# Where TensorE turns the second half of the next chunk in a feed-forward stage

## The reference

```python
def _binarize(w):
    alpha = jnp.mean(jnp.abs(w), axis=1, keepdims=True)
    bw = alpha * jnp.sign(w)
    return w + jax.lax.stop_gradient(bw - w)
def _L0_ffn_ref(x, w1, b1, w2, b2):
    h = jnp.einsum('bsd,hd->bsh', x, _binarize(w1)) + b1
    h = jax.nn.gelu(h, approximate=False)
    return jnp.einsum('bsh,dh->bsd', h, _binarize(w2)) + b2
x = x + 0.5 * _L0_ffn_ref(_layernorm(x), L0_ffn_w1, L0_ffn_b1, L0_ffn_w2, L0_ffn_b2)
```

## Time and profile before

| what | value |
|---|---|
| median of 3 runs | 2248.06 us (2246.12 to 2248.31) |
| the profiled execution's own time | 2251.7 us |
| its span | 2249.8 us |
| PE busy | 1971.8 us (88%) |
| DVE busy | 1643.4 us (73%) |
| ACT busy | 1222.4 us (54%) |
| POOL busy | 497.4 us (22%) |
| `down` of the first block to that of the last, first stage | 52.30 to 178.96 |
| the same, second stage | 694.93 to 818.36 |

### The profile page before, as it was taken

One profiled execution on the slowest core, in us unless ns is written; L12 is line 12 of the kernel. 1 busy time (PEld: TensorE's weight loads), 2 busy tenths in 40 slices (PEclk: granted clock), 3 DMA queues, 4 the chain that ended last, 5 costly groups with the idle time before them and its releaser, 6 DMA issues. The chain is left out here.

```text
span 2249.8 us, 74481 instructions
## 1 busy us (share of the span) xinstructions
PE 1971.8 (88%) x32248; PEld 1256.2 (56%) x32248; DVE 1643.4 (73%) x2668; ACT 1222.4 (54%) x1870; POOL 497.4 (22%) x804
## 2 busy tenths in 40 slices
PE   2897898989897975989869999999999999999985
PEld 2664565656565654558735555555555555555543
DVE  7675556555656778767567888888888888888847
ACT  2673332323236754233227777677776777677754
POOL 3000000000000000000124544345434444445410
PEclk7998999989898976999859999999999999999997
DMA  4000000000000010434583555445453555455312
GB/s 142 1 1 1 21 2 21 3 20 3 20 3 1 1 31 1 132 124 183 186 251 101 143 143 142 130 119 142 128 139 106 142 150 143 116 134 136 100 30 75
DMA packets 273791, 195.11 MB, mean 87 GB/s; under 512 B 206744, under 2 KB 260310, under 8 KB 273210
## 3 DMA queue, kind: packets, MB, share of 16 engines
q1 hardware_dynamic: 262586, 139.27, 24.4%
q0 software_dynamic: 10496, 50.75, 6.0%
q10 hardware_dynamic: 384, 0.33, 0.0%
HBM read 91.69 MB, written 93.88 MB: 82 GB/s over the span
## 5 line engine op out<-in xcount | busy, mean ns | idle before, releaser
L2214 DVE TENSOR_REDUCE a1c_nm<-a1c_S 128x1 f32<-128x1024 f32 x512 | 609.6, 1218 | 84.8 <-PE a1c_S L2301 84.3
L2148 ACT ACTIVATE a1c_PT<-a1c_ST 128x1024 f32<-128x1024 f32 x499 | 510.3, 1023 | 69.0 <-PE a1c_ST L2301 66.2
L2165 ACT ACTIVATE a1c_Pb<-a1c_S,a1c_nm 128x192 f32<-128x192 f32 (+1 forms) x512 | 212.8, 416 | 201.8 <-DVE a1c_nm L2214 200.7
L2087 POOL TENSOR_TENSOR a1c_lt<-a1c_lt 128x256 f32<-128x256 f32 (+5 forms) x448 | 254.7, 568 | 35.4
L2204 DVE COPY a1c_PbT<-a1c_T 96x512 f32<-96x512 f32 x256 | 175.7, 686 | 100.3 <-PE a1c_T L2333 97.9
L2301 PE MATMUL a1c_ST<-a1c_Q,a1c_KR 57*128 57x256 f16 (+2 forms) x1066 | 176.5, 286 | 31.6 <-ACT a1c_PT L2148 19.6
L2301 PE MATMUL a1c_S<-a1c_KL,a1c_Q 54*32 54x512 f16 (+11 forms) x3136 | 193.4, 326 | 0.3
L2301 PE MATMUL a1c_S<-a1c_KR,a1c_Q 54*32 54x512 f16 (+13 forms) x2816 | 181.9, 317 | 12.2 <-DMA a1c_Gx<-a_bias 9.5
L2301 PE MATMUL a1c_S<-a1c_Gx,ident 64*32 64x96 f32 (+2 forms) x4352 | 186.1, 242 | 0.0
L2079 POOL DMA_DIRECT2D a_band<-a1c_Pb x128 | 71.4, 558 | 496.1 <-ACT a1c_Pb L2165 496.0
L1150 POOL PARTITION_ALL_REDUCE b_wall<-b_wsum x2 | 0.8, 407 | 813.3 <-DVE b_wsum L1195 813.3
(11 more groups left out here) (366 smaller groups left out, 3983.1 us busy)
## 6 DMA issues: line engine op xcount, KB each, us to landing
a_band<-a1c_Pb POOLq DMA_DIRECT2D x128, 384.0 KB, 3.5
a_bias<-a1b_G SPq DMA_DIRECT2D x32, 768.0 KB, 9.2
a1c_Gx<-a_bias SPq DMA_DIRECT2D x128, 192.0 KB, 4.4
a1c_Dt<-a_band SPq DMA_DIRECT2D x128, 126.0 KB, 3.7
a1c_Q<-a_qk SPq DMA_DIRECT2D x192, 64.0 KB
a1c_Vw<-a_values SPq DMA_DIRECT2D x64, 102.0 KB, 2.7
a1c_KL<-a_qk SPq DMA_DIRECT2D x96, 64.0 KB
a1c_KR<-a_qk SPq DMA_DIRECT2D x90, 64.0 KB
```

The source lines that it names most:

```text
L2087: add = lambda o, x, y: nc.gpsimd.tensor_tensor(o, x, y, ALU.add)
L2148: nc.scalar.activation(PT[:, q % 8, :, :], place(q), ACT.Exp).then_inc(s["exp"], 1)
L2165: nc.scalar.activation(Pb[:, band_slot(I, c), w0:w1], SP[:, t % 2, I * P - 32 + w0:I * P - 32 + w1], ACT.Exp, bias=nm[:, t // 16 % 2, col: ...
L2214: nc.vector.tensor_reduce(nm[:, t // 16 % 2, col:col + 1], SP[:, t % 2, :], AX.X, ALU.max, negate=True).then_inc(s["max"], 1)
```

## The change

In PE's loop the call that turns the second half of the next chunk stands behind round 2 in place of round 1, that is behind `down(8i + 2)` and `hidden(8i + 5)`. It holds for both stages. Nothing else changes: the waits inside `transposed`, and the lists of ACT and DVE, stay as they are.

```diff
                 if m == MH - 1 and i + 2 < NC:
                     transposed(i + 2, 0)
-                if m == 1 and i + 1 < NC:
+                if m == 2 and i + 1 < NC:
                     transposed(i + 1, 1)
```

## The result

The changed kernel takes 2227.53 us (median of 4 runs, 2224.73 to 2232.91) against 2247.55 (the median with a fourth run of the kernel before): ratio 0.9913, 95% interval 0.9897 to 0.9928. The forecast was 2227.5. Two later measurements gave medians of 2232.19 and 2231.00 us and ratios of 0.9927 (0.9909 to 0.9945) and 0.9919 (0.9901 to 0.9937), so the gain is 17 to 20 us by the medians, and that the first one meets the forecast to 0.03 us is luck.

The account below looks back on a forecast made before the run. PE was taken to bound both FFN stages, not quite full because it pauses at the turn for `xlo`. 17.4 + 3.2 = 20.6 us off the median 2248.06 gave 2227.5 us, range 2223.5 to 2236.5.

Parts of the forecast that it names:

- Step 1: Ordinary chunks of both FFN stages: PE's pause at the second half's turn goes, 1.34 us in each of 13 chunks, 17.4 us.
- Step 2: Rows behind the moved turn (ACT's high part, low part, `hlo` of round 6) still come in time; nothing charged.
- rival 4: Second half too late for the next chunk: ACT's blocked high part delays PE, 5.6 us slower, 2253.7 us; chance 0.03.
- Step 3: First chunk of the first stage: 1.5 us of pause and 1.7 of clock saved, 3.2 us; 1.38 us of pause remain.
- rival 1: Clock still falls in the first stage's first chunk: gain 1.5 + 17.4 = 18.9 us, 2229.2 us; chance 0.22.

## Why the prediction was right

*The bound.* PE sets the pace of both loops, and the pause at the turn was its only one in an ordinary chunk. Shown: with the pause gone PE is busy 14.76 of 14.76 us.

*Step 1, 13 chunks of 1.34 us.* The chunk came out at 14.77 (83.17 - 68.40), the turn at 5.21 into it, the second loop 9.39 us shorter against 7 x 1.34 = 9.38. That the distance between release and place is the cause was shown from both ends: make the release 0.61 later and 0.2 per chunk comes back (so the cover is some 0.4 us, as worked out), make it a block later and everything does.

*Step 2, what is late next.* The 0.95 us between transposes and ACT, and the 1.8 before the next chunk's products, came out as worked (0.95 and 1.82). The `hlo` of round 6 started 77.46 - 68.40 = 9.06 us into the chunk, worked out as 80.78 - 71.64 = 9.14. Moving the turn on showed what these covers are worth: a round more costs nothing, two rounds cost 20.7 us. So rival 4's mechanism is real, and its price was put too low: it let the cost begin at 2.4 us of lateness, which gives 1.1 us a chunk for two rounds (3.47), and the chunk lost 1.63.

*Step 3, the first chunk.* Round 4 at 61.02 against 61.09 worked out; the pause left is 55.70 to 57.10, 1.40 against 1.38. The clock stayed up, as forecast. But the term was mis-sized as a typical gain: 3.2 us holds when the kernel before has its fall there, and that was so in one of its two profiles (two of three, with the kernel that keeps the old first chunk). Where it hasn't, the term is 1.5, and the sum 18.9. All eight profiles in which `down` of round 2 waits there (0.85 to 1.25 us) kept the clock at 1.00 behind it. Taking the upper end, 3.2 us, was right for the one profile it was read from and luck beyond it. In the other case rival 1 has the right sum for another reason: not a fall after the change, but no fall before it.

*Outside the loops.* The three gains by medians, 20.0, 16.9 and 16.6 us, lie at or below the 18.9 to 20.6 of the loops. The stretch between the loops had 515.97 and 518.11 us with the kernel before and 510.2 to 517.2 with the others; from the first turn of the next stage to the end it was 1420.0 and 1418.2 with the kernel before and 1417.2 to 1424.4 with the others. The code there is the same. Where the stretch between was 510.2 the granted clock in it was 0.95, where it was 517 to 518 it was 0.93 and 0.92, so I take the spread for the clock's edges (the times at which it falls and rises), which isn't shown. Whether a microsecond or two of the gain is given back there in general stays open: two profiles of the kernel before don't settle it.

## What to carry to other kernels

When an engine's list is written by hand, look for the place where it waits for a chain that itself started a round ago, and count two distances at once: from the release to the place of the waiting instruction, and from the end of what it issues to whoever needs that next. The good places are those where both are positive; of the four tried here two are, and one further costs all that the first step brings. To judge such an edit, measure the length of the loop in a profile by the starts of its first and last instruction: in three profiles of the changed kernel it repeated to 0.01 us, while the whole times of its 16 runs spread over 11; it was off where a clock edge fell into it (1.7 us in the kernel before) and where its first instruction came late (0.4 us in the kernel with the change in one stage).

## What the runs showed of the hardware

The same pause of 2.8 us of PE (by the starts) went with a fall to the 1.2 GHz level in two profiles (granted clock 0.51 and 0.50) and with none in a third (1.00). Where it came, it came at another time: at 59.8 us in the kernel before, behind the turn, and before 58.4, ahead of the turn, in the kernel with the old first chunk. The eight shorter pauses at that place, of 1.0 to 1.4 us, and the 13 of 1.29 in the first profile were followed by none. The Trainium skill, "TensorE: Matmul & The Clock Gate", section "Part 1: The HAM clock gate", says that the gate's window runs freely and isn't reset by the kernel; by this rule the same pause can cost the clock or not by its place in time. The three profiles agree with that, but none of them shows the window itself. So such a pause has a price with a spread: 0 or 1.6 to 1.7 us here, on top of its own length.
